# First graph layer: residual add on GpSimd, LN1's affine step in ScalarE's copy, LN2's scaling on ScalarE

## The reference

```
def _L0_gnn_ref(x, adj, w_qkv, ln1_g, ln1_b, ln2_g, ln2_b, w1, b1, w2, b2):
    ...
    t = jnp.einsum('fhnm,fmhd->fnhd', attn, v).reshape(F, N, C)   # 8 heads of 16, softmax over the neighbours
    x = _layernorm(x + t, ln1_g, ln1_b)
    h = jax.nn.relu(jnp.einsum('fnc,cd->fnd', x, w1) + b1)
    f_out = jnp.einsum('fnd,dc->fnc', h, w2) + b2
    x = _layernorm(x + f_out, ln2_g, ln2_b)
    return x
...
x = x + _L0_gnn_ref(_layernorm(x, axis=-1), adj, ...)
```

## Time and profile before

| | us |
|---|---|
| median of 3 runs | 1467.51 |
| the runs | 1466.91, 1467.51, 1472.25 |
| the profiled execution | 1470.08 |
| its span | 1468.3 |

### The profile page before, as it was taken

The page is one execution under the profiler, slowest core; times in us unless marked ns, Lnnn a source line. Parts: engine busy times, 40 slices in busy tenths (PEclk is TensorE's granted clock), DMA queues, the critical chain, the costliest instruction groups (busy, mean ns, idle before and its releaser), DMA issues. The chain is left out here.

```text
span 1468.3 us, 31916 instructions
## 1 busy us (share of the span) xinstructions
PE 1180.0 (80%) x8595; PEld 1011.4 (69%) x8595; DVE 1028.1 (70%) x3960; ACT 689.7 (47%) x1768; POOL 870.6 (59%) x742
## 2 busy tenths in 40 slices
PE   6999999578888860999999983667775099999995
PEld 4766676467877750788888872555654089989995
DVE  4999999989888853567777764777675345565554
ACT  5766665246656640333333332544453045555553
POOL 3567666444466776344444441337677658887887
PEclk9999999789889975999999996877796589999998
DMA  6400000000001112566666664223412235555553
GB/s 185 62 2 2 2 2 2 1 1 20 23 32 38 39 44 82 175 194 197 199 199 195 194 188 136 76 82 115 136 59 64 78 55 71 70 65 70 72 67 44
DMA packets 126249, 122.52 MB, mean 83 GB/s; under 512 B 16577, under 2 KB 108097, under 8 KB 126129
## 3 DMA queue, kind: packets, MB, share of 16 engines
q1 hardware_dynamic: 92720, 85.65, 20.9%
q0 software_dynamic: 32960, 35.36, 12.4%
q10 hardware_dynamic: 448, 0.10, 0.0%
HBM read 76.71 MB, written 44.34 MB: 82 GB/s over the span
## 5 line engine op out<-in xcount | busy, mean ns | idle before, releaser
L2847 POOL DMA_INDIRECT out<-m_yb,m_dsti x142 | 229.5, 1616 | 63.7 <-DVE m_yb L2947 23.4
L2141 POOL DMA_INDIRECT rows<-m_yb,m_dsti x135 | 129.2, 957 | 169.6 <-DVE m_dsti L2272 147.9
L1374 POOL DMA_INDIRECT dispatch<-g_flat,g1r_pos x128 | 130.0, 1016 | 73.9 <-issue 32.6
L2217 ACT ACTIVATE m_sg<-psum 128x256 f32<-128x256 f32 (+3 forms) x216 | 79.6, 369 | 178.8 <-PE psum L2170 174.9
L1116 POOL DMA_INDIRECT dispatch<-common_v,a1r_pos x128 | 129.2, 1010 | 52.8 <-issue 36.1
L2170 PE MATMUL psum<-m_xT,m_w 128*128 128x256 f32 (+3 forms) x648 | 140.4, 367 | 0.7 <-ACT m_xT L2208 0.7
L2920 ACT ACTIVATE m_hT<-psum,m_w 128x256 f32<-128x256 f32 (+1 forms) x240 | 92.5, 446 | 100.1 <-PE psum L2874 99.2
L2170 PEld LDWEIGHTS psum<-m_xT,m_w 128*128 128x128 f32 (+1 forms) x648 | 106.5, 178 | 18.0 <-ACT m_xT L2208 0.9
L2885 PE MATMUL psum<-m_w,m_hT 128*128 128x128 f32 x848 | 104.9, 276 | 5.8 <-DVE m_yb L2943 5.8
L2874 PE MATMUL psum<-m_xT,m_w 128*128 128x256 f32 (+1 forms) x480 | 104.1, 361 | 1.0 <-issue 0.8
L2885 PEld LDWEIGHTS psum<-m_w,m_hT 128*128 128x128 f32 x848 | 99.4, 192 | 6.8 <-issue 4.2
(11 more groups left out here) (314 smaller groups left out, 3192.0 us busy)
## 6 DMA issues: line engine op xcount, KB each, us to landing
m_w<-in_c_wall SPq DMA_DIRECT2D x54, 533.0 KB
ahead_w<-in_c_wall SPq DMA_DIRECT2D x18, 533.0 KB, 3.5
g1c_y<-rows SPq DMA_DIRECT2D x32, 256.0 KB, 3.4
m_xg<-dispatch SPq DMA_DIRECT2D x47, 132.0 KB
m_xg<-dispatch SPq DMA_DIRECT2D x46, 130.0 KB, 2.2
resident<-in_c_wall SPq DMA_DIRECT2D x8, 578.0 KB, 5.9
out<-x SPq DMA_DIRECT2D x16, 256.0 KB, 5.6
out<-m_yb,m_dsti POOLq DMA_INDIRECT x142, 3.3
```

The source lines that it names most:

```text
L1374: pool.indirect_dma_start(out=dest, out_offset=bass.IndirectOffsetOnAxis(ap=self.pos[t % 2][:, k, p:p + 1], axis=0), in_=flat[:, p, :], in ...
L2141: pool.indirect_dma_start(out=rows_out, out_offset=bass.IndirectOffsetOnAxis(ap=dsti[j][:, t:t + 1], axis=0), in_=yb[j][:, t, :], in_offse ...
L2217: act.activation(sg[j % 2][0:cn, k, 0:rows], up_banks[j % 2][k][0:cn, 0:rows], ACT.Silu)\
L2847: pool.indirect_dma_start(out=out_rows, out_offset=bass.IndirectOffsetOnAxis(ap=dsti[j][:, t:t + 1], axis=0), in_=yb[j][:, t, :], in_offse ...
```

## The change

VectorE's residual add moves to GpSimd. LN1's gain and shift go into ScalarE's eviction `ffn_T`, as per-partition scale and bias after the transpose (channels lie on partitions there): `ffn_T` transposes LN1's bare output as soon as VectorE has it. The skip `y1b` is now made from the bare output in two GpSimd instructions, with b2 and the shift added together once beforehand. VectorE's `last_norm` becomes four ScalarE instructions at the end of ScalarE's step, for which VectorE makes a small bias `off2` at the end of its own step; groups 14 and 15 keep the form on VectorE. The tile `u` gets two buffers, and GpSimd does the last affine step and the add to `x` one step later. On VectorE `norm(g,0)` now stands ahead of `ffn_stats(g-1)`. On GpSimd `head_rs` stands one step nearer to its use.

```diff
                 def ffn_T(i):                       # scalar
                     if not runs(i):
                         return
+                    if i == 0:
+                        act.wait_ge(early["ffn"], 16 * 10)
                     act.wait_ge(*pe_y1T.now(i))
                     act.wait_ge(*pe_h.before(i))
-                    act.activation(y1T[:, :], bT[:, :], ACT.Copy).then_inc(y1T_ready.sem, 1)
+                    act.activation(y1T[:, :], bT[:, :], ACT.Identity, bias=shift1[:, 0:1], scale=gain1[:, 0:1])\
+                       .then_inc(y1T_ready.sem, 1)
...
+                def last_norm(i):
+                    if not runs(i):
+                        return
+                    act.wait_ge(*off2_ready.now(i))
+                    for p in range(PG):
+                        act.activation(us[i % 2][:, p, :], us[i % 2][:, p, :], ACT.Identity, bias=off2[i % 2][:, p:p + 1],
+                                       scale=rs2[:, p:p + 1]).then_inc(n2_ready.sem, 1)
...
                     probs_T(g, 3)
                     ffn_T(g - 1)
                     head_xn(g + 2)
+                    last_norm(g - 2)
...
-                def ffn_residual(i, b):              # vector
...
-                    dve.tensor_tensor(ts[b][:, :, :], ts[b][:, :, :], xn[i % 4][:, :, :], ALU.add).then_inc(t_ready.sem, 1)
...
+                def last_off(i):
+                    if not runs(i):
+                        return
+                    dve.wait_ge(*rs2_ready.now(i))
+                    dve.wait_ge(*n2_ready.before(i, turns=2))
+                    dve.scalar_tensor_tensor(out=off2[i % 2][:, :], in0=mv2[:, :, 0], scalar=-1.0, in1=rs2[:, :],
+                                             op0=ALU.mult, op1=ALU.mult).then_inc(off2_ready.sem, 1)
...
                     norm(g - 1, 3, 1 - b)
-                    ffn_residual(g - 1, 1 - b)
                     soft(g, 1)
+                    norm(g, 0, b)
                     ffn_stats(g - 1, 1 - b)
-                    norm(g, 0, b)
                     soft(g, 2)
...
                     head_stats(g + 3)
-                    last_norm(g - 2)
+                    last_off(g - 2)
...
                 def step(g, b):                      # gpsimd
-                    ffn_rs(g - 1)
-                    ffn_y1(g - 1, 1 - b)
-                    last_rs(g - 2)
-                    ffn_y1b(g - 1)
+                    residual(g - 1)
+                    last_affine(g - 3)
                     if g == -3:
                         zero_q(0)
-                    head_rs(g + 3)
+                    head_rs(g + 2)
                     if g == -2:
                         zero_v(0)
+                    ffn_rs(g - 1)
+                    last_x(g - 3)
                     if g == -1:
                         zero_q(1)
                         zero_v(1)
                         nobody_rows()
+                    last_rs(g - 2)
+                    ffn_y1b(g - 1)
                     if g == 5:
                         attention.prepare_pool(pool)
-                    last_x(g - 2)
```

More of the change, by code:

```diff
@@ L314, in phase_gnn0 @@
         off = [sb(f"off{i}", [128, PG]) for i in range(2)]
+        off2 = [sb(f"off2{i}", [128, PG]) for i in range(2)]
         xT = sb("xT", [128, GT])
@@ L328, in phase_gnn0 @@
         hT = common["sq"]
-        u = sb("u", [128, PG, C])
+        us = [sb(f"u{i}", [128, PG, C]) for i in range(2)]
         masks = take_semaphore(ctx, nc, "g0_masks")
@@ L512, in ffn_T @@
                         return
-                    pe.wait_ge(*y1_ready.now(i))
+                    pe.wait_ge(*n1_ready.now(i, PG - 1))
                     if runs(i + 2):
@@ L726, in norm @@
                         dve.wait_ge(*y1m.before(i, turns=2))
+                        dve.wait_ge(*pe_y1T.before(i, turns=2))
                     m = rc[:, p % 2, :]
@@ L764, in last_stats @@
                         return
[L765 removed]
+                    norm_stats(dve, lambda p: us[i % 2][:, p, :], st2, mv2, ve2, bn2, ag2, ve2_ready, i, EPS_LN, gate,
                                [u_ready.now(i), rs2_ready.before(i)])
@@ L864, in ffn_rs, with residual, ffn_y1b @@
                     pool.tensor_tensor(rs1[:, :], ve1[:, :], half[:, 0:PG], ALU.pow).then_inc(rs1_ready.sem, 1)
-                def ffn_y1(i, b):
+                def residual(i):
+                    if not runs(i):
+                        return
+                    pool.wait_ge(*o_ready.now(i, PG - 1))
+                    pool.wait_ge(*xn_ready.now(i, PG - 1))
+                    pool.tensor_tensor(ts[i % 2][:, :, :], ts[i % 2][:, :, :], xn[i % 4][:, :, :], ALU.add).then_inc(t_ready.sem, 1)
+                def ffn_y1b(i):
                     if not runs(i):
@@ L869, in ffn_y1, with wait_n2 @@
                     if i == 0:
-                        pool.wait_ge(early["ffn"], 16 * 8)
+                        pool.wait_ge(early["ffn"], 16 * 10)
+                        pool.tensor_tensor(vecs[:, 4, :], vecs[:, 4, :], vecs[:, 1, :], ALU.add).then_inc(shifts, 1)
+                        pool.wait_ge(shifts, 1)
                     pool.wait_ge(*n1_ready.now(i, PG - 1))
-                    pool.wait_ge(*pe_y1T.before(i))
-                    pool.wait_ge(*y1b_ready.before(i))
-                    pool.tensor_tensor(y1[:, :, :], ts[b][:, :, :], vec(0), ALU.mult).then_inc(y1m.sem, 1)
+                    pool.wait_ge(*u_ready.before(i))
+                    pool.tensor_tensor(y1b[:, :, :], ts[i % 2][:, :, :], vec(0), ALU.mult).then_inc(y1m.sem, 1)
                     pool.wait_ge(*y1m.now(i))
[L876 to L883, removed]
+                    pool.tensor_tensor(y1b[:, :, :], y1b[:, :, :], vec(4), ALU.add).then_inc(y1b_ready.sem, 1)
+                def wait_n2(i):
+                    if i < GROUPS - 2:
+                        pool.wait_ge(*n2_ready.now(i, PG - 1))
+                    else:
+                        pool.wait_ge(n2_tail, PG * (i - GROUPS + 3))
                 def last_rs(i):
@@ L888, in last_rs, with last_affine @@
                     pool.wait_ge(*ve2_ready.now(i))
-                    pool.wait_ge(*n2_ready.before(i))
+                    wait_n2(i - 1)
                     pool.tensor_tensor(rs2[:, :], ve2[:, :], half[:, 0:PG], ALU.pow).then_inc(rs2_ready.sem, 1)
+                def last_affine(i):
+                    if not runs(i):
+                        return
+                    wait_n2(i)
+                    u = us[i % 2]
+                    pool.tensor_tensor(u[:, :, :], u[:, :, :], vec(2), ALU.mult).then_inc(fin.sem, 1)
+                    pool.wait_ge(*fin.now(i, 0))
+                    pool.tensor_tensor(u[:, :, :], u[:, :, :], vec(3), ALU.add).then_inc(fin.sem, 1)
                 def last_x(i):
@@ L924, in _ @@
                     step(g, g % 2)
+                residual(GROUPS - 1)
+                last_affine(GROUPS - 3)
                 ffn_rs(GROUPS - 1)
+                last_x(GROUPS - 3)
                 last_rs(GROUPS - 2)
-                ffn_y1(GROUPS - 1, (GROUPS - 1) % 2)
+                ffn_y1b(GROUPS - 1)
                 attend(0, 0, 0)
-                ffn_y1b(GROUPS - 1)
+                last_affine(GROUPS - 2)
                 last_x(GROUPS - 2)
```

46 lines of the change are left out of this document (20 added, 26 removed).

## The result

| | before | after |
|---|---|---|
| median, same chip | 1469.47 (4 runs) | 1486.95 (4 runs) |
| profiled execution | 1470.08 | 1486.26 |

The profiled executions are 16.2 us apart.

The account below looks back on a forecast made before the run. VectorE bounds the kernel at 15.8 us a step, TensorE 1.0 behind. Steady steps +12.9, start -0.15, steps 14 and 15 -3.8, tail -0.9: +8.1 us, so 1475.5 us against the median; range 1463 to 1484.

Parts of the forecast that it names:

- The ring: VectorE's last_off, ScalarE's scalings and ReLU, TensorE's ffn_2 to mix, VectorE's norm(g,0) to next last_off: 16.60 us a step.
- Leg A: Start of VectorE's last_off, through ScalarE and TensorE, to VectorE's norm(g,0): 5.04 us.
- The locks: VectorE's last_off and ffn_norm held by GpSimd instructions reading SBUF: 0.50 us more a step, 16.60 to 17.1.
- the rival without locks: Steps 3 to 13 take 16.6 us with no holding between VectorE and GpSimd: +2.6 us, 1470; chance 0.30.
- the sign named for the locks: L790 (last_off) on VectorE takes some 0.4 us or longer where it meets GpSimd's L899.
- plus 0.9 in step 6: GpSimd's memsets of the next sublayer make ffn_rs and last_x late in step 6: 0.9 us more.
- The start: Up to the steady steps, with norm(2,0) set by TensorE at 51.85 in both kernels: -0.15 us.
- steps 14 and 15: Last two steps, with parts of the attention between: 34.0 us for 37.8 before, -3.8 us.
- The clock rival: TensorE idles near 2 us each step and falls to half clock: 2.6 us more in 11 steps, 1504; chance 0.08.
- The not-slower rival: ScalarE's scalings do not gate the ReLU; TensorE sets steps of 14.8 to 15.1 us, 1454; chance 0.14.

Follow-up runs that it names:

- 1: Changed kernel with ScalarE's four LN2 scalings moved behind probs_T(g,0), one step later; 1474.33 us, ratio 1.0019 to the kernel before.
- 2: Changed kernel with VectorE's norm(g,0) put back behind ffn_stats(g-1); 1471.22 us, ratio 1.0019 to the kernel before.
- 9: Changed kernel with last_off ahead of head_stats on VectorE and GpSimd's memsets moved to step 0; 1466.44 us, ratio 0.9964 to the kernel before.
- 11: Changed kernel with last_off ahead of head_stats, norm(g,0) behind ffn_stats and memsets in step 0; 1460.16 us, ratio 0.9929 to the kernel before.
- 6: Changed kernel with only the swap: GpSimd computes ffn_rs ahead of head_rs; 1491.08 us, ratio 1.0140 to the kernel before.
- 10: Changed kernel with last_off ahead of head_stats, memsets in step 0 and GpSimd's ffn_rs ahead of head_rs; 1471.83 us, ratio 1.0005 to the kernel before.
- 7: Changed kernel with the residual add back on VectorE, behind norm(g-1,3); 1478.87 us, ratio 1.0076 to the kernel before.
- Experiment 4: Changed kernel with GpSimd's memsets for the next sublayer moved from step 5's end to step 0's; 1481.91 us, ratio 1.0093 to the kernel before.
- 3: Changed kernel with LN2's scalings back on VectorE at the end of its step, last_off dropped; 1477.42 us, ratio 1.0076 to the kernel before.
- 5: Changed kernel with LN2's scalings back on VectorE and GpSimd's ffn_rs ahead of head_rs; 1476.66 us, ratio 1.0048 to the kernel before.
- 12: Changed kernel with ScalarE's scalings behind probs_T(g,0), GpSimd's ffn_rs ahead of head_rs and memsets in step 0; 1472.02 us, ratio 1.0020 to the kernel before.

## Why the prediction was wrong in size and right in its main mechanism

- *The ring.* Shown. Leg A measured 5.11 for 5.04. Experiments 1, 2, 9 and 11 each took something out of the ring at another place, and the step fell every time; 6 and 10 put 0.74 in and it grew by 0.74; 7 put work beside it and nothing moved.
- *The locks.* Both there, 0.57 us together for 0.50, so the rival without locks (16.6) fell. One landed elsewhere: on L286 (0.49 for 0.17), the instruction ahead of `last_off`, as L286 came to GpSimd's L899 first; L790 itself took 0.15. The other is L759, 1.35 for 1.11. The step was 17.26 for 17.1; in eleven steps +1.8 us. So the sum was right to 1% here, and the sign named for the locks, a longer L790, did not come.
- *The failing step* is "plus 0.9 in step 6, where GpSimd's memsets ... make `ffn_rs` and `last_x` late". It cost 4.2, +3.3, the largest part of the 8.1 us between the forecast +8.1 and the +16.2 measured. The 0.9 was one wait of 0.96 in the trace of before, whose step grew by only 0.3, as L737 took 0.69 there for 1.42. I looked for lateness on GpSimd; the memsets instead held a VectorE instruction that stands in the ring, and the longer gap then took TensorE's clock. Experiment 4 shows the whole, and 7 the hold without the clock. The trace of before did show the same memsets, and nothing held by them:

```profile
111.46 0.94 POOL L1577 MEMSET a_q<- 128x1024 f32 x1
...
111.69 0.69 DVE L737 TENSOR_TENSOR g_t<-g_t,g_xn 128x512 f32<-128x512 f32 x1
```

- *The smaller terms.* The start was +0.4 for -0.15, steps 14 and 15 took 34.9 us for 34.0: +1.4 together. `last_off` of step 15 was held there, 1.23 us behind a wait of 0.68 for GpSimd, so VectorE's scalings were not the only thing that met GpSimd. With step 6 and the steady steps that is 6.5 of the 6.6 us between the forecast +8.1 and the +14.7 at the layer's end.
- *The rest.* The profiled executions end 16.2 apart, 1.5 more than the layer. What lies behind it is 267.8 to 276.2 us long in these kernels up to the next stage's first weight load, without an edit there, so I give the 1.5 no cause. The kernel before ran at 1469.5 to 1470.7 in the comparisons, 2 to 3 above the 1467.51 to which the forecast was tied.
- *The clock rival* came true in one step of eleven: after 1.72 us idle TensorE stayed at 2.4 GHz, after 3.36 us it was at 1.2, as after 3.27 in 2 and 3.36 in 6. In 7 it stayed at 2.4 GHz after 3.71. So the length of the idle stretch alone did not decide it, and what else did stays open. The forecast priced the clock for all eleven steps or for none. *The not-slower rival* fell with the 3.20 us wait.

That step 6 splits in 1.7 us of holding and 2.2 of clock is read from the rows, and 7 bears it out: with the hold and without the clock's fall it took 19.25, 2.17 us under the 21.42. Some 0.3 of the 4.2 stays open.

## What to carry to other kernels

When work is moved off the bounding engine, walk the longest wait once around all engines before counting the gain: an instruction put in front of one that others wait for can close a ring, and then the engine's spare time is worth nothing. Order alone can open a ring: here `last_off` ahead of `head_stats`, norm(g,0) behind `ffn_stats` and the memsets in step 0 turned +1.1% into -0.7%. What moving the one call `last_off` could give back stood beforehand in the wait that it caused (1.39 us ahead of the scalings, 1.42 gained). One-time work on an engine off the path (memsets in step 6) costs what it meets there, so check it against the instructions that lie in the ring and not against its own engine.

## What the runs showed of the hardware that was not expected

- One VectorE TENSOR_SCALAR of 128x4, 0.17 us alone, was held 2.17 us through five GpSimd memsets in a row (one of 0.20 us, one of 0.11, one of 0.95, and two of 128x528 with 1.02 together); it did not get in between them. The same took 2.18 and 2.19 in experiments 2 and 1, and 2.53 in 3 and 7. In 5 it did get in: it took 1.56 and ended with the third memset, at 114.5, and the two behind it took 1.31 for 1.02. A TENSOR_TENSOR of 128x512 beside the same memset took 0.69 (above), its shortest. The Trainium skill, SBUF — State Buffer, section "Who interferes with whom", makes this difference: an instruction with two SBUF inputs contends only with a GpSimd operation that reads SBUF, one in a 2-port mode with any. The trace agrees for both; that a tensor_scalar of this form is in such a mode no run here shows by itself.
- Four VectorE scalings of 128x128 took 1.11 us free, 1.35 when `last_x` had begun 0.8 us earlier, 1.76 when 0.4 us earlier (11), and 2.06 to 2.09 when both began within 0.2 us (1, 3, 6, 12). The swap, which brought `last_x` from 0.8 us ahead of them to 0.2 behind, moved the step by 0.74 in 6 and in 10.
- A longer idle stretch of TensorE did not always mean a lower clock: 3.27 and 3.36 us were followed by `ffn_2` at the half clock, 3.71 us by `ffn_2` at full clock (7).
